# Two masked linear layers on eight cores: the cached-weight stores issued by ScalarE, after the slab's matmuls, in place of GpSimd

## What is computed

```python
block_mask = mask.reshape(nb, 32, kb, 32).astype(f32).sum(axis=(1, 3)) > 0
w_masked   = weight1 * elem_mask            # the 32x32 blocks whose mask sum is 0 are cleared
x = x + layernorm(layernorm(x) @ w_masked.T)
x = x + layernorm(layernorm(x) @ sign(weight2).T + bias)
```

## Time and profile before

| | us |
|---|---|
| median of 2 runs | 3323.16 (3318.22 to 3328.09) |
| the profiled execution | 3325.92 |
| its span, slowest core (core 1) | 3324.4 |
| spans of the eight cores | 3290.3 to 3324.4 |
| TensorE busy in the span | 2018.8 |
| VectorE busy | 898.1 |
| ScalarE busy | 606.8 |
| GpSimd busy | 362.2 |

### The profile page before, as it was taken

One profiled execution on the slowest core, in us unless ns is written; L12 is line 12 of the kernel. 1 busy time (PEld: TensorE's weight loads), 2 busy tenths in 40 slices (PEclk: granted clock), 3 DMA queues, 4 the chain that ended last, 5 costly groups with the idle time before them and its releaser, 6 DMA issues.

```text
span 3324.4 us, 24248 instructions; the slowest of 8 cores (3290.3 to 3324.4 us)
## 1 busy us (share of the span) xinstructions
PE 2018.8 (61%) x9272; PEld 932.3 (28%) x9272; DVE 898.1 (27%) x1300; ACT 606.8 (18%) x460; POOL 362.2 (11%) x328
## 2 busy tenths in 40 slices
PE   1014133254515555556993997499489948966992
PEld 0011011021212222222441443244234423423440
DVE  0044444534430102043014122400322241022114
ACT  0130000000063333340116001111420021124000
POOL 3555443500000000000000000000000000000000
PEclk9997666676757777777996999699789978977996
DMA  3366676657617777746442454554234445432442
GB/s 127 111 253 240 206 230 219 211 171 227 205 63 235 236 230 245 227 166 238 152 158 85 137 178 141 185 194 152 102 126 178 152 152 202 152 127 76 152 152 101
DMA packets 72946, 573.14 MB, mean 172 GB/s; under 512 B 8800, under 2 KB 8816, under 8 KB 42112
## 3 DMA queue, kind: packets, MB, share of 16 engines
q1 hardware_dynamic: 51840, 343.96, 31.3%
q0 software_dynamic: 18688, 194.08, 16.0%
q10 hardware_dynamic: 2304, 33.56, 2.6%
HBM read 470.86 MB, written 100.70 MB: 172 GB/s over the span
## 4 chain that ended last, share of the span: by engine, by line
PE 42%; DMA 30%; DVE 13%; ACT 9%; issue 4%; POOL 1%; DVEq 0%; ACTq 0%; SPq 0%; POOLq 0%
PE pmm L476 41%; DMA WST<-w1s 11%; DMA WST<-w2s 11%; DVE WSL L395 4%; DMA out<-OS 3%; DMA XS<-x 2%; DVE OS L814 2%; ACT WSL L409 2%; ACT HS L766 2%; ACT HS L735 2%; DVE BNST L595 1%; ACT HT L215 1%; DVE OS L811 1%; DMA OS<-mask 1%; DMA XP<-mask 1%
## 5 line engine op out<-in xcount | busy, mean ns | idle before, releaser
L476 PE MATMUL pmm<-WSL,HT 128*128 128x512 bf16 x8192 | 1890.4, 395 | 736.6 <-DVE WSL L395 265.2
L476 PEld LDWEIGHTS pmm<-WSL,HT 128*128 128x128 bf16 x8192 | 824.1, 101 | 1793.8 <-issue 906.4
L532 DVE TENSOR_TENSOR ARAW<-pmm,BIASF 128x512 bf16<-128x512 f32 x128 | 88.2, 691 | 898.1 <-PE pmm L476 898.1
L395 DVE TENSOR_TENSOR WSL<-WST,BTE 128x1024 bf16<-128x1024 f32 x128 | 244.3, 1924 | 292.4 <-DMA WST<-w1s 291.6
L205 PE MATMUL ptA<-IDN,HS 128*128 128x128 bf16 x576 | 64.7, 302 | 365.9 <-ACT HS L766 236.0
L513 DVE BATCH_NORM_STATS2 BNST<-ARAW 128x6 f32<-128x512 bf16 x96 | 59.3, 680 | 546.0 <-ACT ARAW L503 546.0
L409 ACT ACTIVATE WSL<-WST 128x1024 bf16<-128x1024 f32 x128 | 135.1, 1056 | 245.8 <-DMA WST<-w2s 245.6
L205 PEld LDWEIGHTS ptA<-IDN,HS 128*128 128x128 bf16 x576 | 56.7, 140 | 379.2 <-issue 378.5
L259 POOL TENSOR_TENSOR XP<-XP 128x2048 int32<-128x2048 int32 (+4 forms) x80 | 133.9, 1673 | 108.2 <-DMA XP<-mask 90.8
L503 ACT ACT_TABLE_LOAD x24 | 30.8, 1283 | 497.3 <-PE pmm L476 355.5
L595 DVE BATCH_NORM_STATS2 BNST<-XS 128x6 f32<-128x512 f32 x128 | 78.4, 679 | 153.1 <-DMA XS<-x 153.1
(11 more groups left out here) (61 smaller groups left out, 742.7 us busy)
## 6 DMA issues: line engine op xcount, KB each, us to landing
WSL<-c1m SPq DMA_DIRECT2D x48, 2048.0 KB, 8.6
WSL<-c2m SPq DMA_DIRECT2D x48, 2048.0 KB, 8.4
WST<-w1s SPq DMA_DIRECT2D x128, 512.0 KB, 5.8
WST<-w2s SPq DMA_DIRECT2D x128, 512.0 KB, 4.8
XS<-x POOLq DMA_DIRECT2D x48, 1024.0 KB, 6.0
OS<-mask POOLq DMA_DIRECT2D x16, 2048.0 KB, 9.7
XP<-mask POOLq DMA_DIRECT2D x16, 2048.0 KB, 9.4
c1m<-WSL POOLq DMA_DIRECT2D x16, 2048.0 KB, 10.7
```

Of the source, the lines that this page charges most:

```text
L395: ins = v.tensor_tensor(dst, src, mk, op=OP.mult)
L476: ins = t.matmul(acc_bank(use8, nsl, tt), st_ap, mv_ap, start=(kh == 0 and j == 0), stop=(kh == 1 and j == KTS - 1))
L532: ins = v.tensor_tensor(dst, acc_bank(use8, nsl, tt), BIASF[:, nsl * 512:(nsl + 1) * 512], op=OP.add)
```

## The change

The store of a finished slab moves from GpSimd to ScalarE, and from the preparation of the slab to a place in the loop behind the slab's matmuls, that is, one slab preparation later in program order. `cw_pend` carries slab, layer and the semaphore value that says the slab is finished.

```diff
+        cw_pend = {}
+
+        def emit_cache_write(su):
+            layer, sl, ready = cw_pend.pop(su)
+            buf = WSL[su % 2]
+
+            @blk.scalar
+            def _(s):
+                wt(s, ready)
+                sn = "sC%d" % (su % 2)
+                s.dma_start(cm_d[layer][sl, :, :], buf[:, :]
+                            ).then_inc(sem[sn], 16)
+                cnt[sn] += 16
+                cachew_use[su] = (sn, cnt[sn])
+                cachew_data[(layer, sl)] = (sn, cnt[sn])
...
                 ready = res["m"]
 
-                @blk.gpsimd
-                def _(g):
-                    wt(g, ready)
-                    sn = "sC%d" % (su % 2)
-                    g.dma_start(cm_d[layer][sl, :, :], buf[:, :]
-                                ).then_inc(sem[sn], 16)
-                    cnt[sn] += 16
-                    cachew_use[su] = (sn, cnt[sn])
-                    cachew_data[(layer, sl)] = (sn, cnt[sn])
+                cw_pend[su] = (layer, sl, ready)
...
                         emit_mask_tail(sl // 2 + 2, False)
+                    if su in cw_pend:
+                        emit_cache_write(su)
```

## The result

| | before | changed |
|---|---|---|
| median, us | 3323.9 (15 runs, 3314.11 to 3337.11) | 3338.87 (16 runs, 3326.95 to 3354.35) |
| ratio to before, 95% interval | | 1.0047 [1.0029, 1.0065] |
| spans of the eight cores in the profiled execution | 3290.3 to 3324.4 | 3309.5 to 3349.9 |

The changed kernel is slower, by 15 us or 0.5%. The forecast was 3323, no change; the measured time lies inside the range given (3284 to 3362), but the move is clear of the scatter and was not forecast.

The account below looks back on a forecast made before the run. The prediction took layer 0 of the first chunk as bound by slab making, layer 1 by ScalarE's sign chain. Terms -15 (layer 0), +10 (layer 1) and +4 (its end) sum to -1; forecast 3323 us, range 3284 to 3362.

Parts of the forecast that it names:

- L: Layer 1: landing time of a slab's c2m store from ScalarE, which the first sign waits for; taken as 8 us.
- the layer-1 term: Layer 1, slabs 1 to 15: 14 periods of 28.1 us plus 2 of scatter, 395.4 against 385.8; loss +10.
- The formula around L: Layer 1 slab spacing: period = L + 20.1 us, from table load 1.3 and eight quarters 18.8.
- Layer 0: First chunk's layer 0: less GpSimd waiting starts sums earlier, hiding VectorE stalls; -15 us, bounds -65 and +10.
- The stalls: Layer 0: two or three 17 us VectorE waits would move beside sums, saving 8 us each, 16 to 24 together.
- VectorE's end doesn't move: Layer 0: if only the gaps between sums shrink, VectorE merely loses fast time, so nothing is gained.
- The GpSimd part: Layer 0, between sums of parts: GpSimd waits 46 us less, at most 65; btd wait from 10.9 to 1.8.
- The boundary: End of layer 1: last two stores go together and delay chunk 1's first cached slab; +4 us (0 to +10).
- GpSimd as the true limit of layer 0: Layer 0, faster rival: GpSimd sets the pace, giving -45 us and a total of 3295; chance 0.22.
- The store that holds the sign chain: Layer 1, slower rival: first signs wait a full GpSimd landing, 10.7 to 11.4 us; +47, total 3362; chance 0.20.
- The rule that only issue time is saved: Layer 0 rival: another issuing engine saves only issue time, giving -4 us and a total of 3336; chance 0.10.
- What would show it: Signs: btd wait about 2, slab spacing about 28, landing about 8, slab 7 10 to 25 us sooner; wrong if landing above 10.

Follow-up runs that it names:

- e7: Changed kernel, but SP holds layer 1's first quarter load of slab s+2 until the store of slab s has landed; 3356.12 us, ratio 1.0090 to before.
- e2: Changed kernel with layer 1 put back as before (stores from GpSimd), layer 0 as changed; 3313.38 us, again 3312.34; ratios 0.9981 and 0.9969 to before.
- e3: Changed kernel with layer 0 put back as before (stores from GpSimd), layer 1 as changed; 3348.7 us, ratio 1.0084 to before.
- e8: e1 plus, in layer 0, ScalarE holding an odd slab's store until GpSimd's BTE reads have landed; 3294.35 us, again 3292.25; ratios 0.9924 and 0.9927 to before.
- e9: The kernel of e1 measured once more, beside e8 and e2 on one chip; 3300.0 us, ratio 0.9942 to before.
- e6: Changed kernel, but each late layer-1 store is two 1 MB DMAs with a semaphore each; 3295.66 us, ratio 0.9911 to before.
- e1: Changed kernel, but in layer 1 ScalarE issues a slab's store right behind that slab's own signs; 3304.05 us, ratio 0.9927 to before.

## Why the prediction was right and wrong

**The step that failed** is the size of L in the layer-1 term: "Nearest is the ScalarE row; with one quarter beside it I take 8." The stores landed in 9.0 us on four cores, 8.8 and 9.6 on two and 10.2 and 10.3 on two (medians), and from issue to release it was 9.4 in the mean. The formula around L held: the spacing of 29.2 less 9.4 leaves 19.8 for the rest, where the formula has 20.1, and with halves and L = 6.3 it gave 26.4 against 26.7. So the mechanism, its place and its sign were in the text, and the spacing was put 1.1 us too short, fourteen times: 408.7 us in place of 393.4. The 7.1 of the `out` stores was right for a store that moves alone (6.7 to 7.5 in e7), and 0.9 us was too little for the company: one quarter in flight, and a second that may start as soon as the last sign ends.

A smaller slip is in the same term: I subtracted core 1's own 385.8 us, where the mean of the cores was 381.2. The term came out at +27.5 for +10: 15.3 from the spacing, 4.6 from this slip, less the 2 of scatter that I had added (9.6 before rounding).

**Layer 0** was right in its total, -15 forecast, -16.0 in the changed kernel, -15 in both profiles of e2, but not in all of its working. The stalls did what the text says. Before, on core 1, VectorE's wait for the even slab lies between the end of one part's sums (at 447.94) and the start of the next; in the changed kernel, on core 4, it lies wholly beside them (timelines of DVE and POOL):

```profile
479.68 0.68 DVE L272 TENSOR_SCALAR BRT<-ptB 4x512 bf16<-4x512 f32 x1 [11.75 <-PE ptB L305]
485.57 3.59 POOL L259 TENSOR_TENSOR MHI<-OS 128x2048 int32<-128x2048 int32 x1 [20.52 <-DMA OS<-mask]
```

```profile
457.84 3.59 POOL L259 TENSOR_TENSOR MHI<-OS 128x2048 int32<-128x2048 int32 x1 [13.14 <-DMA OS<-mask]
...
493.11 0.68 DVE L272 TENSOR_SCALAR BRT<-ptB 4x512 bf16<-4x512 f32 x1 [12.22 <-PE ptB L305]
...
506.03 6.81 POOL L259 TENSOR_TENSOR MHI<-MHI 128x1024 int32<-128x1024 int32 x4
```

Of the three such stalls between the sums of parts 4 and 7, none lies beside sums on any core before and in e3 (by more than 2 us), and two of three do on every core in the changed kernel and in both profiles of e2. But two stalls at 8 us would make 16 between slabs 1 and 7, and only 7.8 came there: 7.6 of the 16 us were gained before slab 1 started, where the working has nothing. That gain shows in every kernel with layer 0's stores on ScalarE (slab 1 at 307 to 316 us, against 321 and 325 in before and e3). What makes it wasn't tested, and the good total is in part luck.

The sentence that VectorE's end doesn't move when the gaps alone shrink isn't borne out either. In e8 the same two stalls lie beside sums as in e9, the sums of part 7 end 9 us sooner (596.0 and 605.2, means of the cores), and slab 15 comes 11 us sooner.

The GpSimd part was half wrong as well: the `btd` wait was to fall from 10.9 to 1.8 and fell to 6.5 in the mean (5.6, 3.9 and 10.1 for the three writes), because a store, though on another queue, can be released by the same event. The order of the two kernels shows both waits (`vW`) and I read only the queue. The Trainium skill states the rule that I overlooked ("DMA: Bandwidth & Descriptors", section "Queues, rings and completion order"): a DMA's completion increment is an ordered write that lands only after every earlier write of the same DMA engine, across its queues. The runs agree: 10.7 us with a store on another queue beside it, 4.1 with the store held; they don't tell the rule from plain sharing.

**The boundary** was right in its number and not in its parts. +4 was forecast for the end of layer 1; it cost +3.1 to the first matmuls of chunk 1 and +5.0 behind them, 8.1 in all. Another -3.5, ahead of slab 1 of layer 1, had no term. That the two make +4.6 is luck.

**The rivals.** GpSimd as the true limit of layer 0 was priced at -45. Its waits fell by 27 us in the mean of the cores (3 x 3.3 for the `btd` writes, 4 x 4.4 for the first mask loads of a part), the sums of part 7 ended 28 us sooner, and 16 came out: not the only limit, and the price was far off, though from e9 to e8 its gain came through whole. The store that holds the sign chain was the right mechanism at a price between mine and its own: it "decides from L = 8.1 on", and L was 9.4. The rule that only issue time is saved would give 4 us in layer 0; e2's 15 exclude it, though the store on another queue still held up the small write.

The range's low end was summed as 3325.9 - 45 + 4, with nothing for layer 1, where the text's own bound for a short L is -14; that would make it about 3271. The high end is as it says.

The sum of the terms, taken again with what was measured, is -16 - 3.5 + 27.5 + 8.1 = +16.

**What would show it**, as stated. Came true: the release of the first sign by the c2m store, with 8.9 us in place of some 6; even slabs, at 29 in place of 28; slab 7 sooner by 15 us as the mean of the cores, inside the 10 to 25. Didn't: the `btd` wait of about 2 and the landing of about 8. Two of the signs of being wrong came: a landing above 10, on two cores, and a changed time behind 1450 us, the 5.0 above.

## What to carry to other kernels

When a store moves behind work on an in-order engine, look for the instruction right behind it: if that one waits for the store, the whole landing is on the path, once per turn of the loop, and the store belongs one step earlier or in pieces with a semaphore each. Take the landing from a row with the same traffic beside it, not from a quiet stretch: some 7 us alone became 9 to 10 beside one or two quarter loads. And two DMAs that are released by the same event meet in the DMA engines even on different queues; let the small one that somebody waits for go first.

## What the runs showed of the hardware that I had not expected

- The completion of a 4 KB write took 10.7 us when a 2 MB store had left 0.5 us ahead of it on another engine's queue, and 4.1 (2.2 to 4.7 over three writes and eight cores) with that store held back.
- Two halves of a 2 MB store, issued 0.35 us apart, land with a useful gap: 5.9 to 7.2 us for the first and 8.9 to 9.6 for the second (e6, medians of the cores).
- A DMA behind an operation in one engine's program order can leave while that operation runs: the store is issued 0.07 us after the start of a sign that takes 1.06.
- A 2 MB store landed in 8.8 to 10.3 us from ScalarE (late, medians of the cores) and in 9.4 to 11.7 from ScalarE when issued early, with more loads beside it (e1 and e9); from GpSimd before in 10.1 to 11.4, and in 6.7 to 7.5 from ScalarE with no load beside it (e7). What runs beside a store counts for as much as the issuing engine.
